# Second mixing as three products of rounded values and remainders; more of the shrinking on ScalarE

## What is computed

```python
xf = rfft2(x, axes=(1, 2), norm='ortho').reshape(b, h, wf, 8, 96)      # xr, xi: real, imaginary part
o1r = relu(xr @ w1[0] - xi @ w1[1] + b1[0])                            # per block: 96 to 96
o1i = relu(xi @ w1[0] + xr @ w1[1] + b1[1])
o2r = o1r @ w2[0] - o1i @ w2[1] + b2[0]
o2i = o1i @ w2[0] + o1r @ w2[1] + b2[1]
o2r, o2i = softshrink(o2r, 0.01), softshrink(o2i, 0.01)                # v-l, v+l, or 0 in between
out = irfft2(o2r + 1j * o2i, axes=(1, 2), norm='ortho') + x
```

## Time and profile before

| what | before |
|---|---|
| median of 3 runs | 5124.27 us (5121.58 to 5125.56) |
| span of the profiled execution, its own time | 5120.9 us |
| TensorE matmul, weight load | 98%, 81% of the span |
| VectorE, ScalarE, POOL | 78%, 49%, 12% |
| TensorE's granted clock, mean over the span | 0.999 |
| SP queue, data moved | 411.6 MB |

### The profile page before, as it was taken

How to read it: one execution, slowest core, us unless ns; L and a number is a source line. 1 busy time by engine, 2 the same in 40 slices (tenths; PEclk the granted TensorE clock), 3 DMA queues, 4 the chain that set the end, 5 groups by cost and what they waited for, 6 DMA issues and landing times.

```text
span 5120.9 us, 112005 instructions
## 1 busy us (share of the span) xinstructions
PE 5023.2 (98%) x43200; PEld 4143.8 (81%) x43200; DVE 3992.9 (78%) x5987; ACT 2512.6 (49%) x3649; POOL 626.9 (12%) x420
## 2 busy tenths in 40 slices
PE   7999999999999999999999999999999999999999
PEld 6887878878788887888888888888878878888887
DVE  6778778787787877878777777777787777877877
ACT  4554545545455454554445544545545455454553
POOL 0111011110111101111011110011110111101111
PEclk9999999999999999999999999999999999999999
DMA  3331233312333123332133321333312333123311
GB/s 108 100 102 34 74 101 100 105 44 61 100 100 105 51 55 100 100 105 62 46 98 100 105 77 45 83 100 105 91 44 71 100 105 99 44 63 100 104 51 50
DMA packets 1067748, 421.11 MB, mean 82 GB/s; under 512 B 1064864, under 2 KB 1064992, under 8 KB 1067168
## 3 DMA queue, kind: packets, MB, share of 16 engines
q1 hardware_dynamic: 1062432, 411.63, 30.4%
q10 hardware_dynamic: 4736, 1.60, 0.1%
HBM read 210.26 MB, written 201.33 MB: 80 GB/s over the span
## 4 chain that ended last, share of the span: by engine, by line
issue 88%; POOL 12%; POOLq 0%; DVE 0%
POOL x L948 12%; POOLq L947 0%; POOLq L951 0%; DVE x L877 0%; POOLq L948 0%; POOLq L960 0%
## 5 line engine op out<-in xcount | busy, mean ns | idle before, releaser
L948 POOL TENSOR_TENSOR x<-shrink_or_v,x 128x480 f32<-128x480 f32 (+1 forms) x416 | 626.7, 1506 | 4485.8 <-DVE shrink_or_v L870 4445.1
L549 PE MATMUL ps<-wts,hbig 128*128 128x192 f32 x4160 | 732.1, 327 | 4.3
L842 DVE TENSOR_TENSOR shrink_or_v<-ps,wts 128x768 f32<-128x768 f32 (+1 forms) x544 | 501.1, 921 | 285.3 <-PE ps L558 258.6
L795 DVE COPY ydg<-ps 128x512 f32<-128x512 f32 (+5 forms) x768 | 504.7, 657 | 251.4 <-PE ps L453 151.7
L453 PE MATMUL ps<-tab,ring 128*128 128x128 f32 x6144 | 694.6, 276 | 4.2
L453 PEld LDWEIGHTS ps<-tab,ring 128*128 128x128 f32 x6144 | 688.5, 192 | 10.3 <-DVE ring L916 10.3
L549 PEld LDWEIGHTS ps<-wts,hbig 128*128 128x128 f32 x4160 | 673.2, 190 | 16.3 <-ACT hbig L710 13.7
L440 PE MATMUL ps<-tab,ring 128*64 128x128 f32 x6144 | 680.4, 273 | 3.3 <-ACT ring L650 3.3
L660 ACT COPY ydg<-ps 127x512 f32<-127x512 f32 (+5 forms) x896 | 503.0, 571 | 361.6 <-PE ps L453 185.3
L441 PE MATMUL ps<-tab,ring 128*63 128x128 f32 x6144 | 680.4, 273 | 0.0
L440 PEld LDWEIGHTS ps<-tab,ring 128*64 128x64 f32 x6144 | 671.3, 137 | 7.9 <-ACT ring L650 4.8
(11 more groups left out here) (79 smaller groups left out, 7581.0 us busy)
## 6 DMA issues: line engine op xcount, KB each, us to landing
out<-x SPq DMA_DIRECT2D x352, 480.0 KB, 4.6
x<-in_x SPq DMA_DIRECT2D x192, 768.0 KB, 7.6
x<-in_x SPq DMA_DIRECT2D x32, 816.0 KB, 7.8
x<-in_x SPq DMA_DIRECT2D x32, 720.0 KB, 6.4
out<-x SPq DMA_DIRECT2D x32, 432.0 KB, 4.2
wts<-in_mix SPq DMA_DIRECT2D x16, 513.0 KB, 3.6
out<-x SPq DMA_DIRECT2D x32, 240.0 KB, 4.4
out<-x SPq DMA_DIRECT2D x32, 192.0 KB, 4.3
```

The lines of the kernel that those rows point to most:

```text
L549: mm = pe.matmul(o, hbig[:, k * H:(k + 1) * H], mix_part("w2_big"), start=first, stop=False, skip_group_check=True)
L795: dve.tensor_copy(*line_moves(stage, g)).then_inc(line_dve, 1)
L842: dve.tensor_tensor(parts(v), d, b2, ALU.add).then_inc(bias_done, 1)
L948: pool.tensor_tensor(xs[p][:, a:b, :], ucopy[g % 4][:, 0:b - a, :], mirror(xs[p], a, b), ALU.add).then_inc(plus_ready, 1)
```

## The change

The second mixing becomes three products: remainder of h times rounded w2, rounded h times remainder of w2, rounded h times rounded w2. For that

- ScalarE's relu runs twice for each part, once into an F32R tile (`hbig_hi`, `hsmall_hi`) and once into the F32 tile; the signal comes after the second;
- VectorE subtracts the big part in place (`split_h`), POOL the small part; mix2 waits for these subtractions (`hbig_split`, `hsmall_split`);
- w2 is rounded by ScalarE and its remainder taken by VectorE (`split_w2`), once for every four images, at p = 0 before VectorE's loop turns;
- for the seven wide groups (`SOFT`) the clamp is replaced by a Relu(v - threshold) on ScalarE (`soften`), and VectorE's subtract by min(v + threshold, that). `shrink` is cut in `add_bias` and `shrink`, with split_h, a fold and both halves in a new order;
- mix1 of the last group has a function of its own (`mix1_last`) in another bank, ahead of mix2 of group 8; `early_pack` of the first ring buffer goes behind the last relu;
- the folds are spread over six passes instead of five, two in the first instead of three;
- the ring buffers lie on the upper halves of the mixing buffers.

The diff's core:

```diff
--- before
+++ after
-FOLD_IN = {1: (0, 1, 2), 2: (3,), 3: (4,), 4: (5,), 5: (6,)}
+FOLD_IN = {1: (0, 1), 2: (2,), 3: (3,), 4: (4,), 5: (5,), 6: (6,)}
+SOFT = [p for p in PARTS if len(GROUP_PAIRS[p[0]]) == 4]
+NS = len(SOFT)
...
+        mix_base = nc.sbuf_base
+        sb("mix_area", [128, 6 * 8 * H])
+        def at(name, i, dt=F32, half=0):
+            n = 8 * H // 2 if half else 8 * H
+            return nc.alloc_sbuf_tensor_at(name, [128, n], dt, offset=mix_base + 4 * (8 * H * i + half * 4 * H))
+        zbig = [at(f"zbig{j}", j) for j in range(2)]
+        zhi = at("zhi", 2, F32R)
+        zlo = at("zlo", 3, F32R)
+        hbig = at("hbig", 4)
+        hbig_lo = at("hbig_lo", 4, F32R)
+        hbig_hi = at("hbig_hi", 5, F32R)
+        ring = [at(f"ring{j}", j, half=1)[:].rearrange("p (c k) -> p c k", c=CG) for j in range(RING)]
...
+                def mix1_last(q):
+                    u, n, r = NU - 1, H, SMALL
+                    pe.wait_ge(zbig_ready, NP * q + last_part(u))
+                    pe.wait_ge(zlo_ready, NU * q + u + 1)
+                    pe.wait_ge(zsmall_ready, NU * q + u + 1)
...
+                    pe.matmul(o, lo[1], zhi[:, 0:n], start=True, stop=False)
+                    pe.matmul(o, hi[1], zhi[:, 0:n], start=False, stop=False)
+                    pe.matmul(o, hi[1], zlo[:, 0:n], start=False, stop=False).then_inc(split_read, 1)
...
+                    pe.matmul(os, mix_part("w1_big")[:, BIG:2 * CB], zbig[u % 2][:, 0:n],
+                              start=False, stop=True).then_inc(small_mixed, 1)
...
                 def mix2_whole(q, u):
-                    pe.wait_ge(hbig_ready, NU * q + u + 1)
+                    pe.wait_ge(hbig_split, NU * q + u + 1)
                     n = len(evens(u))
+                    hi, lo = w2_parts(0)
                     for h in range(-(-n // 2)):
                         if set_before(u, h):
                             pe.wait_ge(bias_done, NP * q + set_before(u, h))
                         for o, pair, i, first in mix2_outputs(u, h):
-                            k = i * n + pair
-                            mm = pe.matmul(o, hbig[:, k * H:(k + 1) * H], mix_part("w2_big"),
-                                           start=first, stop=False, skip_group_check=True)
+                            cols = slice((i * n + pair) * H, (i * n + pair + 1) * H)
+                            pe.matmul(o, hbig_lo[:, cols], hi, start=first, stop=False, skip_group_check=True)
+                            pe.matmul(o, hbig_hi[:, cols], lo, start=False, stop=False, skip_group_check=True)
+                            mm = pe.matmul(o, hbig_hi[:, cols], hi, start=False, stop=False, skip_group_check=True)
                     mm.then_inc(hbig_read, 1)
 
                 def mix2_rows(q, u):
-                    pe.wait_ge(hsmall_ready, NU * q + u + 1)
+                    pe.wait_ge(hsmall_split, NU * q + u + 1)
+                    hi, lo = w2_parts(1)
                     for h in range(-(-len(evens(u)) // 2)):
-                        for o, pair, i, _ in mix2_outputs(u, h):
-                            half = slice(i * SMALL, (i + 1) * SMALL)
-                            mm = pe.matmul(o, hsmall[half, pair * H:(pair + 1) * H], mix_part("w2_small")[half],
-                                           start=False, stop=True, skip_group_check=True)
+                        for k in range(len(part_pairs(u, h))):
+                            outputs = [o for o in mix2_outputs(u, h) if o[1] == 2 * h + k]
+                            for z, w, stop in ((hsmall_lo, hi, False), (hsmall_hi, lo, False), (hsmall_hi, hi, True)):
+                                for o, pair, i, _ in outputs:
+                                    half, cols = slice(i * SMALL, (i + 1) * SMALL), slice(pair * H, (pair + 1) * H)
+                                    mm = pe.matmul(o, z[half, cols], w[half], start=False, stop=stop,
+                                                   skip_group_check=True)
                         mm.then_inc(mix2_done, 1)
...
+                            if it == 2 and p == 0:
+                                pe.wait_ge(w2lo_ready, t + 1)
...
+                        mix1_last(q)
                         mix2_whole(q, NU - 2)
                         mix2_rows(q, NU - 2)
-                        mix1_whole(q, NU - 1)
-                        mix1_columns(q, NU - 1)
-                        mix1_rows(q, NU - 1)
                         merge(q)
...
+                    last = u == NU - 1
+                    d = ps[:, Z_BANK:Z_BANK + 1, 0:n] if last else ps[:, BIG_BANK:BIG_BANK + m, 0:n]
+                    ds = ps[0:r, Z_BANK, n:2 * n] if last else ps[0:r, SMALL_BANK, 0:n]
                     act.wait_ge(big_mixed, NU * q + u + 1)
                     if u:
                         act.wait_ge(hbig_read, NU * q + u)
-                    act.activation(hbig[:, 0:m * n].rearrange("p (i n) -> p i n", i=m),
-                                   ps[:, BIG_BANK:BIG_BANK + m, 0:n], ACT.Relu, bias=b1[:, 0:1]).then_inc(hbig_ready, 1)
+                    for h in (hbig_hi, hbig):
+                        mm = act.activation(h[:, 0:m * n].rearrange("p (i n) -> p i n", i=m), d, ACT.Relu,
+                                            bias=b1[:, 0:1])
+                    mm.then_inc(hbig_ready, 1)
                     act.wait_ge(small_mixed, NU * q + u + 1)
                     if u:
                         act.wait_ge(mix2_done, NP * q + last_part(u - 1))
-                    act.activation(hsmall[0:r, 0:n], ps[0:r, SMALL_BANK, 0:n], ACT.Relu,
-                                   bias=b1[0:r, 1:2]).then_inc(hsmall_ready, 1)
+                    for h in (hsmall_hi, hsmall):
+                        mm = act.activation(h[0:r, 0:n], ds, ACT.Relu, bias=b1[0:r, 1:2])
+                    mm.then_inc(hsmall_ready, 1)
+                def soften(q, u, h):
+                    at = part_at(u, h)
+                    n = halves(u) * len(part_pairs(u, h)) * 2 * CB
+                    act.wait_ge(bias_done, NP * q + at)
+                    if at > 1:
+                        act.wait_ge(shrunk, NP * q + at - 1)
+                    act.activation(clamped[:, 0:n], biased[at % 2][:, 0:n], ACT.Relu,
+                                   bias=minus_lambd[:, 0:1]).then_inc(soft_done, 1)
...
+                            for i, name in enumerate(("w2_big", "w2_small")):
+                                mm = act.copy(w2s[:, i, 0, :], mix_part(name))
+                            mm.then_inc(w2hi_ready, 1)
                         for it in range(NU + 1):
                             if it < NU:
                                 for h in range(2):
                                     if (it, h) in PARTS:
                                         copy_big(q, it, h)
+                                    if (it - 3, h) in SOFT:
+                                        soften(q, it - 3, h)
                                 round_big(q, it)
                                 round_small(q, it)
-                            if it == NU:
-                                early_pack(q, 0)
                             if it >= 1:
                                 relu(q, it - 1)
+                        early_pack(q, 0)
                         early_pack(q, 1)
...
+                def split_w2(t):
+                    dve.wait_ge(w2hi_ready, t + 1)
+                    for i, name in enumerate(("w2_big", "w2_small")):
+                        mm = dve.tensor_tensor(w2s[:, i, 1, :], mix_part(name), w2s[:, i, 0, :], ALU.subtract)
+                    mm.then_inc(w2lo_ready, 1)
...
+                def split_h(q, u):
+                    n = halves(u) * len(evens(u)) * H
+                    dve.wait_ge(hbig_ready, NU * q + u + 1)
+                    dve.tensor_tensor(hbig_lo[:, 0:n], hbig[:, 0:n], hbig_hi[:, 0:n],
+                                      ALU.subtract).then_inc(hbig_split, 1)
+                def add_bias(q, u, h):
+                    (pairs, m, ne, n), at = part_sizes(u, h), part_at(u, h)
+                    v = biased[at % 2][:, 0:n].rearrange("p (k i c) -> p i k c", i=m, c=2 * CB)
...
                     dve.wait_ge(mix2_done, NP * q + at)
+                    if at > 2:
+                        dve.wait_ge(shrunk, NP * q + at - 2)
                     else:
                         dve.wait_ge(y_ready, NF * q + NF)
+                    dve.tensor_tensor(v, d, b2, ALU.add).then_inc(bias_done, 1)
+                def shrink(q, u, h):
+                    (pairs, m, ne, n), at = part_sizes(u, h), part_at(u, h)
+                    v, c = biased[at % 2][:, 0:n], clamped[:, 0:n]
...
+                    if (u, h) in SOFT:
+                        dve.wait_ge(soft_done, NS * q + at)
+                        if first:
+                            dve.scalar_tensor_tensor(edge[:].rearrange("p i c -> p (i c)"), v[:, 0:cut], LAMBD,
```

(77 more changed lines are left out.)

20 lines of the change are left out of this document (9 added, 11 removed).

## The result

The changed kernel takes 5514.42 us (median of four, 5509.8 to 5516.59), the kernel before 5124.92 us beside it: ratio 1.0758, 95% interval 1.0745 to 1.0771. That is 389 us more, where 246 (5370 - 5124) were forecast, and 4 us above the range. The profiled execution spans 5508.0 us.

The account below looks back on a forecast made before the run. The prediction took the matrix engine, busy 98% of the span, as the bound. Its terms, 42+136+46+24 = 248 us on the profiled 5120.9, with the runs' median 3 above, gave 5370 us; forecast 5290 to 5450 (0.62), wider range 5230 to 5510.

Parts of the forecast that it names:

- Term 1: Second mixing: three F32R products, each spaced 0.112 us by its weight load, 0.336 against 0.326 now; +1.3 us an image, 42 us.
- Rival (a): Second mixing's weight load is hidden or fast, so products cost their columns; 5155 at 0.09 us, 5090 at 0.083; chance 0.08.
- (d): Under 256 columns a rounded product streams at half rate, 0.16 us each: +470, 5840 us; chance 0.03.
- Term 2: Longer way from first to second mixing: doubled relus and the tail stall TensorE 4.25 us an image, 136 us.
- rival (b): Covered hand-overs between the mixings: small stalls absorbed, only 37 us of them left; 5250 us; chance 0.15.
- rival (c): Hand-over chain becomes the bound: shrink waiting for soften makes remainder late in every wide pass; +208, 5580 us; chance 0.10.
- T+3.92: Forecast end of split_h in wide passes, T being mix1_rows' end; mix2_whole arrives at T+5.6, cover 1.7 us.
- fits behind the 1.14: Group 0: without late folds, split_h adds no wait beyond the first wide pass's relu stalls of 1.01 and 0.13 us.
- Term 3: Behind VectorE's jump, folds start 4.3 us late, so mix2_whole waits for split_h: +3.3 us in 14 images, 46 us.
- Term 4: TensorE's longer idles lower its clock to 1.2 GHz in nearly all of 14 images, 1.7 us each: 24 us (0 to 50).

Follow-up runs that it names:

- run 76: Not a run's number: 76 us at the lower clock level, in the changed kernel with 32 memsets ahead of VectorE's loop; 5427.63 us.

## Why the prediction was wrong

The direction, the chain and most of the places were right; the size failed in one term above all. Per other image, by the mean starts of the stages:

| stretch of an image | forecast, us | measured, us |
|---|---|---|
| first wide pass, relus ahead of mix1 | 1.14 | 1.20 |
| first wide pass, mix2_whole waits for split_h | 0 | 0.67 |
| products of that pass | 0.16 | 0.19 |
| five wide passes, products and relus | 1.85 | 1.98 |
| half-wide pass | 0.82 | 0.82 |
| last pass and tail | 1.55 | 1.87 |
| lines and rows, where images meet | 0 | 1.02 |
| sum | 5.5 | 7.75 |

**Term 1, right.** 0.112 us a product, from weights of 128 against 64 in the earlier trace rows, stood to the third digit, and the runs with half the columns and half the weights show the reason. Rival (a) fell with it: F32R loads of 128 weights do not go faster than these rows. So did (d), 0.16 a product.

**Term 2, right in the mixing, short at the ends.** Relus and products cost what was worked out, and the run with early-freed banks shows that it is the signal after the second relu, not ScalarE's longer work. So rival (b), that the stalls are absorbed, did not come true, nor did rival (c), the chain over shrink and remainder: TensorE doesn't wait for zsmall_lo. Two slips in the sums change nothing: split_h ends at T+3.96 by its own terms, not T+3.92, and the upper bound of term 1 is 98 x 0.034 = 3.3, not 3.6.

Two steps failed here. In group 0 split_h was to be one that "fits behind the 1.14" at 1.22 us; this forgot that POOL's subtraction starts half a microsecond earlier and reads the same memory: split_h takes 2.31 there, and mix2_whole comes 0.67 late. (That "split_h is costed at nothing in wide passes" held in the five that follow, where mix2_whole never waits for it.) POOL's work was priced by its own duration only, while VectorE's row should have been doubled where the two meet. And 1.02 us an image where images meet was not seen. Half of it is TensorE waiting 0.67 us instead of 0.14 at row 0 of every second image, for the last sums of VectorE. The other half lies in the forward lines of the images with odd q, whose weight loads wait for ScalarE's copies to `ring`: 8.5 of the 11.6 us below, and none of the 4.8 before (rows of all images, before and then after):

```profile
PEld ps L440 <- ACT ring L650: 4.8, 7, 1.9
```

```profile
PEld ps L470 <- ACT ring L707: 11.6, 36, 1.9
```

No run took these two apart, so what makes VectorE and ScalarE late there stays open. Together these and the tail are 2.2 us in 18 images, 40 us.

**Term 3, the failed step.** "the folds start late: 60.0/14 = 4.3 us on the mean" was taken over as a constant of the jump. It went with where the loop's code lies. The change altered VectorE's program and moved its loop; the first fold came to lie one instruction packet further behind the jump's target, and the lateness became 10.2 us. The shifts by 32 to 96 memsets bring it back to 3.3 to 3.5 us and the time to some 5429 us, inside the forecast's own 5290 to 5450. The late images then lose 3.8 us more than the others do (11.5 against 7.7 us), where terms 3 and 4 had forecast 5.0 (70/14): with the short wait the chain costs no more than was worked out. The prediction's sum with 10.2 for 4.3 would have been 5370 + 14 x 5.9 = 5453. Of the 144 us between forecast and result this is 86. That a late packet takes so long is the loads' doing (4.2 us for two packets without them, 10.2 with them), and that it costs TensorE all of it is the chain as predicted: folds, split_h, mix2_whole. A smaller term was off too: split_w2 takes 0.6 us, not 0.3, and runs at each jump, that is once for every two images (not four, as the list of the change has it).

The Trainium skill has the rule ("Runtime: NRT & Kernel Launch", "Instruction fetch mechanics"): a taken branch whose target isn't held forces a fetch before the engine can go on. The waits of the earlier trace rows and all 14 of the changed kernel agree with it, and the prediction read them only as a number. Their price in these runs is 3.3 to 3.5 us on the mean for one packet beside loads, 4.2 for two without loads and 10.2 for two beside them.

**Term 4, right in kind.** All 14 images lose the clock, as forecast. The cost was put at 1.7 us each; mix2_whole alone takes 5.05 us instead of 2.85 there, so with an idle time of some 10 us it is at least 2.2.

Of the remaining 18 us or so (144 - 86 - 40), 5 are the start: the first matmul comes 34.2 us into the span instead of 29.1. Most of the rest lies in the late images, which even with the short wait lose 1.0 us each more than forecast (11.5 against 5.5 + 5.0); this was not taken apart.

## What to carry over

A wait for nothing that the profile names, right behind an engine's jump, was instruction fetch here: its size went with where the code lay and with what the DMA engines carried, and an edit of that engine's program can change it, as 32 memsets did, so give it a range of one packet more, and see who stands first behind the jump. Writing the loop out over more turns was a cheap remedy, worth 11 us even where the wait was mostly covered. And a subtraction given to POOL was not free for VectorE: where both read SBUF at once (2.31 us instead of 1.22), count one after the other.

## What the runs showed of the hardware that was not expected

- The wait behind VectorE's jump, on the mean: 3.3 to 3.5 us for one instruction packet while loads run, 10.2 us for two, 4.2 us for two without loads. 32 tiny instructions ahead of the loop moved the time by 87 us.
- Fewer moving columns brought a lower clock: with 96 instead of 192, in one execution, TensorE was at its lower level for 406 us instead of 171, some of it behind stretches in which it was busy for 0.92 of the time.
- TensorE came out of an idle time of 9.7 to 11.0 us with the lower clock in 14 of 14 images, of 4.0 to 4.6 us in 14 of 14 too (with 32 memsets; without the end of the run 76 us at that level instead of 158), of up to 2.0 us in the kernel before in 1 of 14.
